# A conditioned attention and convolution kernel: the preparation stage rewritten, and the stores that follow it placed elsewhere

## What is computed

```
def attention_block(x, emb, W_emb, b_emb, g_norm, W_qkv, g_q, g_k, W_out):
    scale_shift = emb @ W_emb + b_emb                 # (4, 1, 2048)
    scale, shift = split(scale_shift, 2)
    xn = rms_norm(x, g_norm) * (1.0 + scale) + shift
    q, k, v = heads(xn @ W_qkv)                       # 16 heads of 64
    q, k = rms_norm(q, g_q), rms_norm(k, g_k)
    attn = softmax(q @ k.T * 64 ** -0.5)
    o = (attn @ v).reshape(b, n, dim)
    return o + o @ W_out
x = x + attention_block(x, cond, ...)
x = x + causal_depthwise_conv(x, taps=cond, b_conv)   # four taps, one for each batch row of cond
```

## Time and profile before

| what | value |
|---|---|
| median of three executions | 2493.46 us (2492.73 to 2496.19) |
| profiled execution, its own time | 2493.3 us |
| its span in the profile | 2491.5 us |
| `prepare` ends, first VectorE instruction of `main` | 95.9 us |
| TensorE busy | 2380.8 us, 96% of the span |
| VectorE, ScalarE, GpSimd busy | 84%, 73%, 26% |

### The profile page before, as it was taken

One profiled execution on the slowest core, in us unless ns is written; L12 is line 12 of the kernel. 1 busy time (PEld: TensorE's weight loads), 2 busy tenths in 40 slices (PEclk: granted clock), 3 DMA queues, 4 the chain that ended last, 5 costly groups with the idle time before them and its releaser, 6 DMA issues.

```text
span 2491.5 us, 54548 instructions
## 1 busy us (share of the span) xinstructions
PE 2380.8 (96%) x20950; PEld 1572.6 (63%) x20950; DVE 2098.6 (84%) x3369; ACT 1816.1 (73%) x2827; POOL 635.4 (26%) x444
## 2 busy tenths in 40 slices
PE   6799988998899999999999999999999999999899
PEld 6555555555466666666666666666666666666678
DVE  7868988888878888888888888888888888888876
ACT  3467888887877778777777787777777777777632
POOL 0023233322332222323322233223212222222100
PEclk9999999999999999999999999999999999999999
DMA  8989989999998999999998999999988998888961
GB/s 354 286 231 224 192 172 191 187 180 226 194 201 181 197 193 201 184 199 223 199 214 183 212 178 201 189 188 226 202 175 170 181 173 163 170 166 165 178 189 52
DMA packets 1234227, 485.01 MB, mean 195 GB/s; under 512 B 1139505, under 2 KB 1196977, under 8 KB 1231537
## 3 DMA queue, kind: packets, MB, share of 16 engines
q1 hardware_dynamic: 1233968, 481.53, 91.2%
HBM read 137.99 MB, written 56.66 MB: 78 GB/s over the span
## 4 chain that ended last, share of the span: by engine, by line
PE 66%; DVE 17%; issue 5%; ACT 3%; SPq 2%; DMA 2%; POOL 1%; ACTq 0%; POOLq 0%
PE proj L903 33%; PE scores L844 10%; PE values L863 9%; PE proj L928 8%; DVE neg L1425 8%; DVE p_pair L1434 5%; ACT p_pair L1082 2%; SPq L674 2%; DMA w_sb<-w_dram 1%; DVE bias L1428 1%; PE proj L933 1%; PE misc L945 1%; ACT late L1074 1%; PE values L878 1%; PE misc L915 1%
## 5 line engine op out<-in xcount | busy, mean ns | idle before, releaser
L903 PE MATMUL proj<-w_sb,xn_sb 128*128 128x384 f16 x6144 | 1036.0, 328 | 25.3 <-DMA w_sb<-w_dram 15.4
L1074 ACT ACTIVATE late<-scores,bias,l_scale 128x1024 f32<-128x1024 f32 x512 | 615.6, 1203 | 347.2 <-DVE bias L1428 328.2
L903 PEld LDWEIGHTS proj<-w_sb,xn_sb 128*128 128x128 f16 x6144 | 588.3, 98 | 429.5 <-issue 25.1
L1434 DVE TENSOR_TENSOR p_pair<-late,p_pair 128x1024 f16<-128x1024 f32 x512 | 616.3, 1245 | 122.8 <-ACT p_pair L1082 122.6
L1425 DVE TENSOR_REDUCE neg<-scores 128x1 f32<-128x1024 f32 x512 | 623.1, 1217 | 111.5 <-PE scores L844 108.1
L1082 ACT ACTIVATE p_pair<-late 128x1024 f16<-128x1024 f32 x512 | 511.0, 1050 | 0.0
L863 PE MATMUL values<-pT,v_pair 128*64 128x256 f16 x6144 | 390.9, 278 | 15.8 <-ACT inv_row L1138 12.6
L844 PE MATMUL scores<-late 64*128 64x512 f16 x3072 | 376.8, 378 | 16.6 <-ACT late L1074 14.8
L863 PEld LDWEIGHTS values<-pT,v_pair 128*64 128x64 f16 x6144 | 320.0, 111 | 95.7 <-issue 74.2
L1343 POOL TENSOR_TENSOR rs<-ms,power 128x16 f32<-128x16 f32 x63 | 183.1, 2906 | 404.1 <-DVE ms L1448 403.7
L928 PE MATMUL proj<-late,wo 128*128 128x256 f16 x2304 | 267.7, 273 | 0.4 <-issue 0.4
(11 more groups left out here) (168 smaller groups left out, 2077.7 us busy)
## 6 DMA issues: line engine op xcount, KB each, us to landing
w_sb<-w_dram SPq DMA_DIRECT2D x124, 384.0 KB, 4.2
o_dram<-oT_pair SPq DMA_DIRECT2D x124, 128.0 KB, 2.4
out<-late SPq DMA_DIRECT2D x54, 256.0 KB, 2.8
x_in<-in_x SPq DMA_DIRECT2D x25, 512.0 KB, 4.6
late<-in_x SPq DMA_DIRECT2D x25, 512.0 KB, 3.9
wq_raw<-in_L_cond_W_qkv SPq DMA_DIRECT2D x8, 1536.0 KB, 10.8
late<-o_dram SPq DMA_DIRECT2D x12, 1024.0 KB, 6.2
xn_dram<-late SPq DMA_DIRECT2D x21, 512.0 KB, 3.3
```

The costliest lines, as they stand in the source:

```text
L903: last = nc.tensor.matmul(proj[:, t % 2, 0:6 * DH], xn_sb[:, t, i * K + c, :], w_sb[:, c, j, :], start=(c == 0 and i == j == 0), stop=(c = ...
L1074: nc.scalar.activation(prob[:, h, :], scores[:, h, :], ACT.Exp, bias=bias[:, s:s + 1], scale=const["l_scale"][:, 0:1], accum_out=total[:, ...
L1434: nc.vector.tensor_tensor(p_pair[:, s % 4, 1, :], prob[:, h, :], p_pair[:, s % 4, 0, :], ALU.subtract).then_inc(lo_done, 1)
```

## The change

**W_emb.** It is issued by ScalarE on its own queue, between its instructions. The condition (128 rows, 4 columns) is now the loaded weight and W_emb passes 512 columns at a time, four matmuls for each chunk. The result is 4 rows of 2048; ScalarE copies it out of PSUM and 16 transposes turn it back.

**Scales of chunks 1, 3 and 5.** These come from the sum of squares of a row, made by ScalarE with one `Square` over 3072 columns, and a maximum and a power on GpSimd, in place of VectorE's maximum over the row.

**Modulation.** The rows are broadcast before they are scaled by their maximum, chunks 0 to 6 first and chunk 7 later; the scaling is applied in the high and low halves of the first eight x blocks. GpSimd raises the row factors in two parts, the second of them in `main`.

**Buffers and stores.** `wq_raw` has four buffers. Chunks 1 and 2 are made in the tile `wo`. `prepare` stores only chunks 0 and 3 to `w_dram` and copies all eight parts to `w_sb`. Chunks 4 and 5 are stored between the transposes of `main`, chunk 1 after them; once the first projection is done, seven DMAs fill `w_sb` for unit 1, then chunks 2, 7 and 6 are stored, and then `load_x` follows.

```
@@ prepare: SyncE
+            def load_wq(c):
+                need(sp, wq_lo, c - 3)
+                sp.dma_start(wq_raw[:, c % 4, :], wq_v[c]).then_inc(wq_in[c % 4], 16)
+            def first_w(c):
+                sp.wait_ge(wq_lo, c + 1)
+                sp.dma_start(shared["w_sb"][:, c]..., pair_of(c)[:, 0]...).then_inc(w0_in, 16)
...
-            load_emb(0)
-            load_wq(1)
-            load_emb(1)
-            load_wq(2)
-            for c in range(3, K):
-                load_emb(c - 1)
-                if c == K - 1:
-                    load_emb(c)
-                load_wq(c)
-                if c == 3:
-                    keep_wq(0)
-                if c >= 4:
-                    for v in (2 * c - 8, 2 * c - 7):
-                        sp.dma_start(first_x[v], x_t[v * P:(v + 1) * P, :]).then_inc(x_in[v // 4], 16)
-            for c in range(1, K - 2):
-                keep_wq(c)
+            for c in range(1, 4):
+                load_wq(c)
+            for c in range(4, K):
+                load_wq(c)
+                first_w(c - 4)
+                if c in (5, 6):
+                    load_x(2 * c - 10)
+                    load_x(2 * c - 9)
+            for v in range(4, K):
+                load_x(v)
+            keep_wq(0)
+            keep_wq(3)
+            for c in range(4, K):
+                first_w(c)
+            sp.wait_ge(wq_out, 32)
@@ prepare: GpSimd
+            for i, c in enumerate(by_sums):            # by_sums = (1, 3, 5)
+                pool.wait_ge(wq_sq, i + 1)
+                nc.gpsimd.tensor_scalar(wq_ss[:, c:c + 1], wq_ss[:, c:c + 1], TINY, None, ALU.max).then_inc(wq_floor, 1)
+                pool.wait_ge(wq_floor, i + 1)
+                nc.gpsimd.tensor_tensor(wq_max[:, c:c + 1], wq_ss[:, c:c + 1], const["power"][:, 0:1], ALU.pow)...
             pool.wait_ge(top_in, 1)
             nc.gpsimd.partition_all_reduce(topr[:], top[:], P, RMAX).then_inc(top_all, 1)
             pool.wait_ge(x_ms, 1)
-            nc.gpsimd.tensor_tensor(shared["x_rs"][:], x_ss[:], const["power"][:, 0:K], ALU.pow)
+            nc.gpsimd.tensor_tensor(x_rs[:, 0:4], x_rs[:, 0:4], const["power"][:, 0:4], ALU.pow)
@@ prepare: ScalarE
+            def load_emb(c):
+                need(act, emb_mm, c - 1)
+                nc.scalar.dma_start(emb_w[:, c % 2, :], emb_v[c]).then_inc(emb_in[c % 2], 16)
+            def wq_squares(c):
+                act.wait_ge(wq_in[c % 4], 16 * (c // 4 + 1))
+                nc.scalar.activation(dump[:], wq_raw[:, c % 4, :], ACT.Square,
+                                     accum_out=wq_ss[:, c:c + 1]).then_inc(wq_sq, 1)
...
+            load_emb(0)
+            load_emb(1)
+            high(0)
+            load_emb(2)
+            wq_squares(1)
+            high(1)
+            load_emb(3)
+            high(2)
+            load_emb(4)
+            wq_squares(3)
+            load_emb(5)
+            high(3)
+            load_emb(6)
+            high(4)
+            load_emb(7)
+            wq_squares(5)
+            high(5)
+            act.wait_ge(emb_mm, K)
+            nc.scalar.activation(erow, ps_e[0:B, :], ACT.Copy).then_inc(emb_row, 1)
+            high(6)
+            for v in range(4):
+                x_square(v)
+            read_rows(0, K - 1, 0)
+            for v in range(4, 6):
+                x_square(v)
+            high(7)
+            read_rows(K - 1, K, 2)
+            for v in range(6, K):
+                x_square(v)
@@ prepare: TensorE
-                for m in range(2 * K):
-                    last = nc.tensor.matmul(ps_t[:, m * B:(m + 1) * B], emb_w[:, c % 2, m * P:(m + 1) * P], cT[:, c, :],
+                for n in range(4):
+                    last = nc.tensor.matmul(ps_e[0:B, n * 512:(n + 1) * 512], cT[:, c, :],
+                                            emb_w[:, c % 2, n * 512:(n + 1) * 512], start=(c == 0), stop=(c == K - 1))
...
+            pe.wait_ge(emb_row, 1)
+            for m in range(2 * K):
+                last = nc.tensor.transpose(ps_e[:, m * B:(m + 1) * B], erow[:, m * P:(m + 1) * P],
+                                           const["eye32"][0:B, 0:B])
+            last.then_inc(emb_t, 1)
...
             pe.wait_ge(mod_done, 1)
+            broadcast(0, K - 1)
+            pe.wait_ge(mod_done, 2)
+            pe.wait_ge(mod_cp, 2)
+            broadcast(K - 1, K)
@@ prepare: VectorE
-            for c in range(1, K):
-                scale_of(c)
-                if c < K - 1:
-                    lows_of(c - 1)
-            v.wait_ge(emb_mm, K)
+            lows_of(0)
+            scale_by_sums(1)
+            scale_by_maximum(2)
+            lows_of(1)
+            lows_of(2)
+            scale_by_sums(3)
+            scale_by_maximum(4)
+            lows_of(3)
+            lows_of(4)
+            scale_by_sums(5)
+            scale_by_maximum(6)
+            lows_of(5)
+            v.wait_ge(emb_t, 1)
...
+            weigh(0, K - 1)
+            scale_by_maximum(7)
+            weigh(K - 1, K)
...
-            lows_of(K - 2, range(1))
+            lows_of(6)
+            x_mean(0)
             v.wait_ge(top_all, 1)
...
+            lows_of(7)
+            x_mean(4)
@@ main: SyncE, the head
-            for c in range(K - 2, K):
-                sp.dma_start(w_sb[:, c]..., late_chunk(late, c, K)[:, 0]...).then_inc(w0_in, 16)
             for v in range(K):
                 transpose_x(v, first_pair[v % 4], xn_sb[:, v], xn_in[v])
-            for c in range(K - 2, K):
-                sp.dma_start(w_dram[:, :, c]..., late_chunk(late, c, K)...).then_inc(late_out[1], 16)
-            for i in range(4):
-                load_w(1, i)
+                if v == 1:
+                    keep_late(FRONT)
+                if v == 3:
+                    keep_late(FRONT + 1)
+            keep_wo(1)
+            sp.wait_ge(qkv_mm, K)
+            second_w(0, 1, w_dram[1, :, 0:1])
+            second_w(1, 2, wo_chunk(const["wo"], 1, K)[:, 1:2])
+            second_w(2, 3, wo_chunk(const["wo"], 2, K)[:, 1:2])
+            second_w(3, 4, w_dram[1, :, 3:4])
+            sp.wait_ge(late_out[0], 32)
+            second_w(4, 6, w_dram[1, :, 4:6])
+            for c in (6, 7):
+                second_w(c, c + 1, late_chunk(late, c, K)[:, 1:2])
+            keep_wo(2)
+            for c in (7, 6):
+                keep_late(c)
             load_x(K)
@@ main: TensorE, project
+                        pe.wait_ge(w0_in, 16 * K)
+                    elif t == 0 and w == 1 and c == 0:
+                        pe.wait_ge(w1_in, 16 * (K - 1))
@@ main: the first eight x blocks
+                    nc.scalar.activation(pair_[:, 0], buffer, ACT.Copy, scale=const["mod_up"][:, 0:1])...
-                nc.vector.tensor_tensor(first_pair[v % 4][:, 1], first_x[v], first_pair[v % 4][:, 0], ALU.subtract)...
+                nc.vector.scalar_tensor_tensor(out=first_pair[v % 4][:, 1], in0=first_x[v],
+                                               scalar=const["mod_up"][:, 0:1], in1=first_pair[v % 4][:, 0],
+                                               op0=ALU.mult, op1=ALU.subtract)...
```

More of the change, by code:

```diff
@@ L366, in _ @@
             step(nc.vector.reciprocal(twoi[:], two[:]))
[L367 removed]
+            step(nc.vector.tensor_scalar(up[:], twoi[:], X_UP, None, ALU.mult))
             for i in range(2):
@@ L648, in load_w @@
                 need(sp, qkv_mm, K * w)
-                if w == 1:
-                    for i_ in range(2):
-                        sp.wait_ge(late_out[i_], 32)
                 passed()
```

238 lines of the change are left out of this document (135 added, 103 removed).

## The result

The changed kernel is slower: 2501.97 us median of 7 executions (2500.01 to 2506.95) against 2492.73 of the kernel before in the same runs (2490.13 to 2496.19); ratio 1.0039, 95% interval 1.0029 to 1.0049, which is 7 to 12 us. The forecast was 2491, its range 2479 to 2499. The profiled execution took 2506.95 us, the longest of the seven, with a span of 2505.1, 13.6 above; the medians are 9.2 apart, so the profile shows some 4 us more loss than the typical execution has.

A forecast was written before the change was run, and what follows sets the result against it. TensorE's chain bounds the kernel, behind a preparation that is a race of VectorE and the DMA queue ending in a barrier. Terms: -17.0 + 3.7 + 10.7 = -2.6 us, giving 2491 us, range 2479 to 2499.

The forecast's parts named there:

- new waits on VectorE: In the preparation: waits for new scales, W_emb buffers, the row's copy and transposes, and chunk 7's highs, together 5.9 us.
- work left: In the preparation: VectorE's work of 70.2 us falls to 60.7 once three maxima go and small steps are added.
- first maximum: In the preparation: VectorE's first maximum starts at 11.9 instead of 8.95, since W_emb's loads share the DMA engines.
- the front: The preparation up to main's first x block: that block begins at 79.0 against 96.04, 17.0 us earlier.
- saved maxima: In the preparation: three of VectorE's maxima go, 3 x 3.35 = 10.1 us of its work.
- half of the old product for a chunk: In the preparation: TensorE's W_emb product per chunk, taken as 3.5 us, with bounds of 5.8 and 6.9.
- second rival: In the preparation: ScalarE held by its own DMA issues, front gain only 7, end 2500.7 us; chance 0.1.
- stretch behind the row: End of the preparation: row copy and transposes after W_emb's last chunk charged 0.8 us, chunk 7's highs behind x squares 1.3.
- first eight x blocks: Start of main: transposes 2 and 4 land 1.2 and 2.3 us late behind stores; cost 3.7 us, between 0 and 5.
- ninth block: In main: x load 11.9 us later behind three stores, TensorE stalls 9.2 and resumes cold; cost 10.7 us, between 7 and 13.
- first rival: In main: the ninth x block does not stall, so -17.0 + 3.7 = -13.3, end 2480.0 us; chance 0.2.
- the third: In the preparation: DMA stays at 355 GB/s, block begins near 89, end 2500.7 us; chance 0.06.

The follow-up runs named there:

- e7: The changed kernel with chunks 1, 3 and 5 of W_qkv scaled by their maximum on VectorE again; median 2499.6 us, ratio 1.0039 to the kernel before.
- e3: The changed kernel with W_emb issued by SyncE among W_qkv's chunks, ScalarE issuing none of it; median 2499.0 us, ratio 1.0039 to the kernel before.
- e6: The changed kernel with all x loads behind W_qkv's last chunk and products of constants keeping TensorE busy; median 2499.3 us, ratio 1.0039 to the kernel before.
- e5: The changed kernel with all eight x loads issued behind W_qkv's last chunk; median 2502.0 us, ratio 1.0043 to the kernel before.
- e14: e13 with the stores of e8 in the stretch of idle DMA engines; median 2485.1 us, ratio 0.9965 to the kernel before.
- e17: e14 with chunk 5's store alone moved behind the first transposes of main; median 2481.2 us, ratio 0.9959 to the kernel before.
- e2: The changed kernel with the stores of chunks 4 and 5 issued after all eight transposes; median 2496.6 us, ratio 1.0030 to the kernel before.
- e4: The kernel before, with three added 1.57 MB stores to a spare tensor ahead of its ninth x block; median 2504.1 us, ratio 1.0056 to the kernel before.
- e8: The changed kernel storing chunks 1, 2, 4, 5 at the front's end, 6 and 7 behind the first transposes; median 2487.8 us, ratio 0.9983 to the kernel before.
- e11: The changed kernel with work moved ahead of W_emb's row, e8's stores and e6's products of constants; median 2490.7 us, ratio 0.9997 to the kernel before.
- e13: The changed kernel with work moved ahead of W_emb's row and chunk 7's highs ahead of the broadcast's copies; 2497.9 us, ratio 1.0017 to the kernel before.

## Why the prediction was wrong

**The step that failed: the new waits on VectorE, 5.9 us.** They were 16.2: 1.5, 0.8 and 2.0 for GpSimd's powers, 5.0 for ScalarE's highs of chunk 4, which stood behind the wait for a W_emb buffer, 6.9 for the row. The work left (60.7; measured 88.8 - 12.2 - 16.2 = 60.4) and the first maximum (11.9; 12.2) were right, and the old waits for W_qkv went as forecast. The waits are 10.3 of the 10.8 us that the front fell short; most of the rest is the step from VectorE's end to the next block (1.0 for 0.5). I treated the saved maxima as saved time because VectorE was the longest list; e7 shows that putting them back costs nothing. What came last was a chain I had only as small charges, W_emb's: its last load was issued at 52.39 and its product ended 16.5 us later, at 68.9. The cold clock is a smaller part of that: I had counted it in `main` alone and took half of the old product for a chunk (3.5), which is right at 2.4 GHz (3.60), while at 1.2 GHz it is 6.8 (eight records 0.85 apart); at the end of the chain that cost at most some 2.6 us. The second rival, ScalarE held by its own issues, is excluded by their length, 0.33 to 0.46 us each; what held it were the waits for a buffer in front of them, and e3 shows that taking those away gains nothing by itself. What remains is two buffers, each refilled in about 10 us from engines that are full, and the odd one refilled 6.2 us late at 24.16. e6's rows show that chain link by link, but what would shorten it is argued: I ran nothing with a third buffer or with chunk 3 issued earlier, and e5 did not resolve what the traffic ahead costs. The Trainium skill ("DMA: Bandwidth & Descriptors", on issuing engines not being separate queues) says that DMAs of any issuer interleave on the same 16 engines; this trace agrees, with W_emb's 1.05 MB landing in 10.3 us at a total of 415 GB/s, by which 1.05 MB alone would take 2.5 (an estimate).

**The stretch behind the row**, charged 0.8 and 1.3, took 7.0 more than before. Some 3 to 4 of it was order (e14's VectorE 3.7 less behind the product, e17's front 3.2 less): chunk 7's maximum behind the row, and its highs behind the broadcast's copies.

**The first eight x blocks, 3.7**: right. TensorE waited 1.18 and 2.83 (forecast 1.2 and 2.3); e2's profile has 4.3 less.

**The ninth block, 10.7**: the mechanism was right and is shown twice (e4 puts it into the old kernel, e8 takes it out of the new). Landing 13.3 us later for 11.9, TensorE idle 10.5 for 9.2, cold behind it: 12.8 in all, counted to the third scores (172.16 against 161.48, 10.7, and the 2.1 by which the first projections were ahead). SyncE also needed 4.97 us to issue the three stores and 3.46 for the load itself, where the earlier trace rows has 0.33.

**The sum**: -6.2 + 4.1 + 12.8 = +10.7 at the third scores, against -2.6 forecast; the medians say +9.2. The two profiled executions are 13.6 apart: 3 us more are lost right behind the third scores, where the next weights were waited for 3.07 us (before 1.75) and their first 24 matmuls took 5.74 (before 4.30). The sum has no term for that. The first rival (no stall) is excluded by the trace, the third (a mean rate of 355 GB/s) by 409 to 422 GB/s in the full stretch: its front, near 89, came about by another way. Both slower rivals price the end at 2500.7, close to the 2502.0 measured; that is luck, for neither mechanism is in the trace. My range was too narrow on the slow side, since I gave the chain behind the DMA no rival of its own.

**Open**: why W_emb's last product ends anywhere between 62.8 and 69.8 with the same or nearly the same program (its last load is issued between 49.6 and 53.9); e11's loss in units 1 to 3.

## What to carry to other kernels

Work taken from the longest engine is worth only what the next chain leaves: follow the last transfer through its product, its copy and all that the program orders behind it before counting the saving. A store that nobody waits for has a price by its place in an ordered queue, both in what lands late behind it and in the issuing engine's own time; look for the stretch in which the DMA engines are idle, and then check that the issues themselves do not hold a barrier. In each engine's list put what has its data ahead of what waits; a load whose buffer is free is late by all that its issuer waits for in front of it (6.2 us for chunk 3 of W_emb).

## What was not expected of the hardware

An issue on SyncE's queue, 0.33 us when little is outstanding, took 4.34 for two stores (DMA share 0.96) and 14.19 for one (e17, at 51.34, share 1.02), so in these rows the issuing engine is itself held by the backlog. The products of constants kept TensorE at its full clock over a preparation in which its real work is sparse (1.00 against 0.69 to 0.76), and no gain in time can be told (e6 1.0039, e5 1.0043). GpSimd's idle time between all-reduce and power was 7.70 us, as before the change (7.66); with the power ahead of the all-reduce (e13) it lay under VectorE's work and cost nothing.
